# Third attention layer of a four-layer model: context projections ahead of the loop by way of DRAM, values one batch early, heads turned seven steps behind

## What is computed

```
ln_out = _ln(hidden_states, ln_w, ln_b)
q = _ln(_fp8_linear(ln_out, wq), qln_w, qln_b)      # 16 heads of 128
k = _ln(_fp8_linear(ln_out, wk), kln_w, kln_b)      # 8 heads of 128
v = _fp8_linear(ln_out, wv)                         # 8 heads
core = _gqa(q, k, v)                                # softmax(q k^T / sqrt(128)) v
qx = _ln(_fp8_linear(ln_out, wqx), qxln_w, qxln_b)
kvx = einsum('bsi,oi->bso', cond, w_kv_x)           # cond: the context, in f32
kx, vx = split(kvx, 2)                              # kx gets a layer norm per head
core_x = _gqa(qx, kx, vx)
y = fp8_linear(concat(core, core_x) * smoothing, wproj)
```

## Time and profile before

| | |
|---|---|
| median of the runs | 1834.83 us |
| the profiled execution, its own time | 1835.48 us |
| span, first to last instruction | 1833.7 us |
| PE busy | 1525.9 us (83%) |
| DVE busy | 1080.1 us (59%) |
| ACT busy | 804.5 us (44%) |
| POOL busy | 794.2 us (43%) |
| mean granted clock of TensorE | 0.871 |
| L2 attention, rounding stage | 864 to 899 us |
| L2 attention, main loop | 899 to 1307 us |

### The profile page before, as it was taken

One profiled execution on the slowest core, in us unless ns is written; L12 is line 12 of the kernel. 1 busy time (PEld: TensorE's weight loads), 2 busy tenths in 40 slices (PEclk: granted clock), 3 DMA queues, 4 the chain that ended last, 5 costly groups with the idle time before them and its releaser, 6 DMA issues. The chain is left out here.

```text
span 1833.7 us, 25059 instructions
## 1 busy us (share of the span) xinstructions
PE 1525.9 (83%) x8562; PEld 980.8 (53%) x8600; DVE 1080.1 (59%) x2317; ACT 804.5 (44%) x1879; POOL 794.2 (43%) x959
## 2 busy tenths in 40 slices
PE   7566659999797799997399999999799989836772
PEld 5222235656464365655167777777455555525661
DVE  7999961223674643355778888888722255462336
ACT  3989862110333211112488888888521112412221
POOL 3367641000200299791277777777210000027772
PEclk9655659999697999998699999999899988858796
DMA  2499871110504011320200000000111100156656
GB/s 78 89 177 182 172 162 33 36 42 18 184 2 167 27 48 65 115 66 25 68 2 1 1 1 1 1 1 1 44 30 43 35 25 1 46 195 233 231 171 238
DMA packets 174223, 140.12 MB, mean 76 GB/s; under 512 B 141793, under 2 KB 154721, under 8 KB 170386
## 3 DMA queue, kind: packets, MB, share of 16 engines
q1 hardware_dynamic: 165314, 114.89, 22.0%
q0 software_dynamic: 6416, 22.03, 3.6%
q10 hardware_dynamic: 2368, 1.61, 0.3%
HBM read 85.43 MB, written 19.50 MB: 57 GB/s over the span
## 5 line engine op out<-in xcount | busy, mean ns | idle before, releaser
L389 PE MATMUL l1e_gu<-x_normT,l1e_w 128*128 128x512 f32 x384 | 171.6, 602 | 0.0
L1859 POOL CAST l0m_pi<-l0m_pf 128x1024 bf16<-128x1024 int16 x128 | 133.2, 1040 | 87.0 <-ACT l0m_pf L1926 85.4
L1451 PE MATMUL l2x_pr<-l_w,l2x_xq 128*128 128x512 bf16 x538 | 133.6, 385 | 37.8 <-ACT credits L42 35.9
L1926 ACT ACTIVATE l0m_pf<-l0m_s,l0m_bias,l0x_sq 128x1024 int16<-128x1024 f32 x128 | 153.9, 1204 | 19.2 <-DVE l0m_bias L1957 12.6
L1953 DVE TENSOR_REDUCE l0m_mx<-l0m_s 128x1 f32<-128x1024 f32 x128 | 155.6, 1215 | 4.7 <-PE l0m_s L1868 4.4
L1868 PE MATMUL l0m_s<-l0x_kT,l0x_qT 64*128 64x512 bf16 x256 | 70.6, 575 | 64.7 <-ACT l0m_pf L1926 63.5
L389 PE MATMUL l0e_gu<-x_normT,l0e_w 128*128 128x512 f32 x272 | 121.3, 601 | 0.0
L1578 DVE BATCH_NORM_STATS2 l2x_bn<-l2x_raw 128x6 f32<-128x128 f32 x384 | 83.3, 279 | 64.3 <-ACT l2x_raw L1519 64.3
L389 PEld LDWEIGHTS l1e_gu<-x_normT,l1e_w 128*128 128x128 f32 x384 | 74.2, 194 | 84.2 <-issue 83.1
L389 PE MATMUL l2e_gu<-x_normT,l2e_w 128*128 128x512 f32 x256 | 114.3, 602 | 0.0
L441 ACT ACTIVATE l1e_sil<-l1e_gu 128x512 f32<-128x512 f32 x48 | 28.6, 596 | 178.6 <-PE l1e_gu L389 178.6
(11 more groups left out here) (505 smaller groups left out, 3608.1 us busy)
## 6 DMA issues: line engine op xcount, KB each, us to landing
l3m_w<-in_l_moe SPq DMA_DIRECT2D x16, 1280.0 KB, 6.9
l1e_w<-in_l_ffn SPq DMA_DIRECT2D x24, 384.0 KB, 3.1
l_rows<-zero_row SPq DMA_DIRECT2D x8, 1024.0 KB, 10.9
l_w<-l_rows SPq DMA_DIRECT2D x8, 1024.0 KB, 12.7
l0e_w<-in_l_ffn SPq DMA_DIRECT2D x17, 384.0 KB, 3.1
l2e_w<-in_l_ffn SPq DMA_DIRECT2D x16, 384.0 KB, 3.1
ctx_tok<-l_route SPq DMA_DIRECT2D x8, 512.0 KB
l2q_wps<-in_l_wp SPq DMA_DIRECT2D x16, 256.0 KB, 2.8
```

The costliest lines, as they stand in the source:

```text
L389: last = nc.tensor.matmul(gu[half][:, m, :], w[:, c % SW, (2 * k + m) * P:(2 * k + m + 1) * P], pg.xnT[:, k, cols(n)], start=(k == 0), sto ...
L1451: last = nc.tensor.matmul(flat(pr[t % 2][:]), src[:, k, tokens], pg.l2_w3[:, part, k, at:at + W], start=(k == 0 and part == 0), stop=(k == ...
L1859: nc.gpsimd.tensor_copy(pi[:, n % 8, :], pf[:, n % 4, :]).then_inc(s["rounded"], 1)
L1926: nc.scalar.activation(pf[:, n % 4, :], s_ps[n % 3][:], ACT.Exp, scale=sq[:, h, b:b + 1], bias=bias[:, n % 4:n % 4 + 1], accum_out=sm[:, b ...
```

## The change

- **Context projections move.** PE computes all 32 of them (8 batches, four parts of 512 columns: kx twice, vx twice) in the rounding stage, into eight PSUM banks. ACT copies each to one of four buffers `kv`, one behind each copy of output weights, and the last 18 after the rounds. POOL stores each to the DRAM tensor `l2_kv`.
- **SP loads them in the loop**, four loads of 256 KB per batch, into `kx` and `vx`, two batches deep, which lie where the weights `l2_wx` were.
- **Values one batch early.** Side 1 used steps 0 and 1 for kx and 6 and 7 for vx. Now its steps 0 and 1 project the v of the next batch, so steps 6 and 7 are without projection in every item but the first. The last item has none in steps 0 and 1 either. Statistics and normalization of kx read `kx` instead of `raw`.
- **Heads are turned at lag 7** instead of 6 on PE and ACT.

The diff, cut to its core:

```diff
+            @block.tensor
+            def _(pe):
+                for i in range(KV_STEPS):
+                    b, u = divmod(i, 4)
+                    if i >= 8:
+                        pe.wait_ge(kv_kept, i - 7)
+                    for k in range(KD):
+                        last = nc.tensor.matmul(kv_ps[i % 8][:], pg.ctxT[:, k, b * P:(b + 1) * P], pg.l2_wx[:, k, u * W:(u + 1) * W],
+                                                start=(k == 0), stop=(k == KD - 1))
+                    last.then_inc(kv_done, 1)
+
+            @block.gpsimd
+            def _(pool):
+                for i in range(KV_STEPS):
+                    pool.wait_ge(kv_kept, i + 1)
+                    pool.dma_start(pg.l2_kv[i], kv[:, i % 4]).then_inc(kv_stored[i % 4], 16)
+
+                def keep_kv(i):
+                    act.wait_ge(kv_done, i + 1)
+                    if i >= 4:
+                        act.wait_ge(kv_stored[i % 4], 16 * (i // 4))
+                    nc.scalar.activation(kv[:, i % 4], kv_ps[i % 8][:], ACT.Copy).then_inc(kv_kept, 1)
...
                             keep(q)
+                            keep_kv(q)
                 keep(14)
                 keep(15)
+                for i in range(14, KV_STEPS):
+                    keep_kv(i)
...
+            def source(it, t):
+
+                if t >= 6 or (it[1] == 1 and t < 2):
+                    return V_, it[0] + it[1], t % 2
+                return (QX if it[1] else K_ if t < 2 else Q_), it[0], None
+
+            def projects(it, t):
+                if it is None:
+                    return False
+                if t >= 6:
+                    return it == (0, 0)
+                return it != (B - 1, 1) or t >= 2
...
+            @block.sync
+            def _(sp):
+                for b in range(B):
+                    for i in range(4):
+                        sp.wait_ge(kv_stored[i], 16 * (b + 1))
+                    if b >= 2:
+                        sp.wait_ge(s["normed"], item((b - 2, 1)) * 6 + 2)
+                    for u in range(2):
+                        sp.dma_start(kx[:, b % 2, u], pg.l2_kv[4 * b + u].rearrange("p (j d) -> p j d", j=U)).then_inc(kx_in[b % 2], 16)
+                    if b >= 2:
+                        sp.wait_ge(s["valued"], item((b - 2, 1)) * 4 + 4)
+                    for u in range(2):
+                        sp.dma_start(vx[:, b % 2, u * W:(u + 1) * W], pg.l2_kv[4 * b + 2 + u]).then_inc(vx_in[b % 2], 16)
...
-                        if job := norm_due(t, 6, pi, ai):
+                        if job := norm_due(t, 7, pi, ai):
...
-                            dve.wait_ge(s["raw"], item(pi) * 8 + t + 3)
+                            if source(pi, t)[0] != V_:
+                                dve.wait_ge(s["raw"], projected(pi, t) + 3)
+                                rows = raw[:, t]
+                            else:
+                                dve.wait_ge(kx_in[pi[0] % 2], 16 * 2 * (pi[0] // 2 + 1))
+                                rows = kx[:, pi[0] % 2, t]
```

More of the change, by code:

```diff
@@ L1283, in attention_l2 @@
         wp_in = [pg.sem(f"l2q_wp_in{i}") for i in range(4)]
+        kv_done, kv_kept = pg.sem("l2q_kv_done"), pg.sem("l2q_kv_kept")
+        kv_stored = [pg.sem(f"l2q_kv_stored{i}") for i in range(4)]
+        KV_STEPS = 4 * B
         with ExitStack() as st:
@@ L1292, in attention_l2 @@
             wps = sb("wps", [P, 4, 2, D])
+            kv = sb("kv", [P, 4, W])
+            kv_ps = [st.enter_context(nc.psum_tensor(f"l2q_kv_ps{i}", [P, W], F32)) for i in range(8)]
             block = st.enter_context(nc.Block())
@@ L1441, in fn @@
                     for t in range(8):
[L1442 to L1457 removed]
+                        if projects(pi, t):
+                            pe.wait_ge(s["raw"], projected(pi, t) + 1)
+                            which, batch, part_v = source(pi, t)
+                            tokens = slice(batch * P, (batch + 1) * P)
+                            src = xq[:, which]
+                            at = 3072 + part_v * W if which == V_ else 4096 + (t - 2) * W if which == QX else t * W
+                            for k in range(KD):
+                                for part in range(3):
+                                    last = nc.tensor.matmul(flat(pr[t % 2][:]), src[:, k, tokens], pg.l2_w3[:, part, k, at:at + W],
+                                                            start=(k == 0 and part == 0), stop=(k == KD - 1 and part == 2))
                             last.then_inc(s["proj"], 1)
@@ L1512, in fn @@
                     for t in range(8):
[L1513 to L1519 removed]
+                        if projects(pi, t):
+                            act.wait_ge(s["proj"], projected(pi, t) + 1)
+                            which, batch, part_v = source(pi, t)
+                            dst = pg.xnT[:, batch % 2, part_v * W:(part_v + 1) * W] if which == V_ else flat(raw[:, t])
+                            nc.scalar.activation(dst, flat(pr[t % 2][:]), ACT.Copy, scale=scales[:, which:which + 1]).then_inc(s["raw"], 1)
                         if job := due(t, 3, ai, zi, wi):
```

51 lines of the change are left out of this document (21 added, 30 removed).

## The result

The changed kernel takes **1848.72 us** (median of 4 runs, 1846.66 to 1851.12), the kernel before 1835.04 beside it (4 runs, 1834.25 to 1835.59): a ratio of 1.0071, 95% interval 1.0058 to 1.0085. It is 13.7 us slower. 1821 was forecast, with 1805 to 1836 as the range.

What follows compares the result with a forecast made beforehand. PE was taken to bound the loop, every microsecond counting (24.35 us per item). +22.9 (rounding stage) - 2.8 - 5.7 - 23.9 - 4.3 (loop items) = -13.8 us, giving 1821 us, range 1805 to 1836.

Steps and rivals of the forecast that it cites:

- items 3 to 14: Steady main loop: 22.4 us per item instead of 24.39, together -23.9 us.
- PE's own work: Main loop: PE's work falls to 20.9 us per item, the lower bound of an item.
- The free steps: Steps 6 and 7, without projections: PE waits for ACT's copy of turned probabilities, 0.8 to 0.95 us beyond PE's work.
- DVE and POOL late for step 0: Steps 4 to 7 into step 0: late DVE statistics and POOL rstd delay the normalization of probabilities, 0.6 us per item.
- Meetings of DVE and POOL: Main loop: DVE and POOL block each other on the shared port more often, at most another 0.5 us per item.
- rival C: Loop steps 4 to 7: DVE and POOL become the bound; slower from 23.55 us per item, 1845 at 24.4; chance 0.13.
- The rounding stage: Ahead of the loop: 32 projections take 55.0 us of PE at full clock; stage 58.8 against 35.9 us, +22.9.
- D: Rounding stage: stores set the pace, ACT waiting for buffers and PE for banks; 10 us more, 1831; chance 0.12.
- E: Rounding stage: lower clock throughout, 110 us for the projections, +55 on the sum, 1876; chance 0.05.
- About 1 us at either end: Ends of the rounding stage: hand-over to the next block, about 1 us, beside the last copy and last store issue.
- Item 0 and items 1 and 2: Loop start: item 0 falls from 13.6 to 10.8 us (-2.8), items 1 and 2 from 43.15 to 37.5 (-5.7).
- Item 15: Last item: without projection in steps 0 and 1, 20.9 us instead of 25.2, -4.3; the end behind it stays.

Runs made afterwards that it cites:

- e11: Changed kernel with statistics of two of four heads (less DVE) and POOL's power made a product, together: 1829.32 us (one run), pair of items 43.96 us.
- e5: Changed kernel with less DVE work: statistics of two of four heads from the third item on; 1843.20 us (one run), pair of items 46.11 us.
- e6: Changed kernel with less POOL work: the power in the rstd sets becomes a product; 1834.74 us (one run), pair of items 45.13 us.
- e7: Changed kernel with less ACT work: four scaled copies of the output heads become one instruction; 1843.63 us (one run), pair of items 46.03 us.
- e8: Changed kernel with less PE work: one of four matmuls of each output part; 1851.67 us (one run), pairs of 46.87 to 48.38 us.
- e3: Changed kernel with the 32 stores issued from SP's queue instead of POOL's: 1843.70 us, ratio 1.0036 to the kernel before.
- e13: Kernel before with only the heads turned seven steps behind instead of six: 1834.97 us, ratio 0.9996 to the kernel before.
- e4: Changed kernel with only the 16 context value projections moved, keys projected in the loop: 1827.69 us, ratio 0.9956 to the kernel before.
- e9: Changed kernel with only the 16 context key projections moved, values projected in the loop: 1824.38 us, ratio 0.9933 to the kernel before.
- e1: Changed kernel with heads turned at lag 6 again instead of 7: 1849.61 us, ratio 1.0063 to the kernel before.

## Why the prediction was wrong

The step that failed is **items 3 to 14**, "22.4 per item", and in it the term for what comes late to step 0, "I put 0.6 on this". It measured 1.5 (1.16 for POOL, as foreseen, and 0.36 for ACT's copy of turned heads, not foreseen). The mechanism was right in the main and the term mis-sized: 0.9 of the 1.0 us per item that were missing. The item is half of the whole error: 12.3 of the 25 us between -13.8 and +11.4.

- *PE's own work*, 20.9 per item, held: e11, with DVE and POOL lightened, comes to 21.98 with one wait of 0.62 left, 0.8 in all; the remaining 21.2 is 0.3 above it.
- *The free steps*, "0.8 to 0.95 beyond PE's work": named rightly, the values' wait for ACT's copy is there in every item, 0.62 listed and about 0.8 in all. I took it from the end of the loop, where the listed wait is 0.69. One reading there was wrong: in the pair of steps that took 4.26 PE doesn't wait for probabilities but for ACT's copy of turned heads (below). Two similar sizes from two causes made it look like one.
- *DVE and POOL late for step 0*, "I put 0.6 on this": the place and the queue were right (POOL's normalization of probabilities, behind the third rstd set). The size was 0.97 listed, 1.16 in all, and 0.36 for the copy of turned heads beside it: 1.5. I showed no row for it and put a small number. The end of the loop before has rows of both waits, which I passed over; they show the places and not the size:

```profile
1281.57 0.63 PE L1471 MATMUL l2x_tr<-ident,l2x_raw 128*128 128x128 f32 x4 [0.52 <-ACT l2x_qT L1533]
1297.45 0.66 PE L1478 MATMUL l2x_pt<-ident,x_norm 128*128 128x128 f32 x4 [0.26 <-POOL x_norm L1434]
```

- *Meetings of DVE and POOL*, "at most another 0.5 per item": DVE's busy time over ten items of the steady loop is 207.0 us (1013.9 to 1248.4), before 204.4 (991.2 to 1234.7), so 0.3 per item.
- *The range of the sum*. The break-even that I worked out for rival C, 23.55 per item, was 1.15 above my value, a twentieth of an item; it got 0.13. What came is 23.44 without a bound engine. I had tied the slow outcome to "DVE and POOL become the bound"; it needs neither full (e5 to e8). That a chain over four engines is a little late at several links fits all but e8's side of it, and is argued, not shown.

*The rounding stage* (+22.9 forecast, +25.5): the 55.0 us of matmuls came out at 55.2 (866.93 to 922.1), at full clock, and neither ACT nor the stores held them; D and E fell, and a store took 2.3 us in the median (3.9 beside the rounding), issued in 0.54. The missing 2.6 us is the hand-over. "About 1 us at either end" assumed that a stage ends when its last DMA is issued; e3 shows that on POOL's queue it ended 3.3 us later.

*Item 0 and items 1 and 2* (-8.5 forecast, -4.0): PE's gap at the hand-over was 5.49 us, not 3, and the clock fell again (0.87 to 940), 1.8 us by e3; and items 1 and 2 pay the waits that the others pay, and once 1.73 for ACT's copy of turned heads (at 951.85).

*Item 15* (-4.3 forecast, +2.5): the sum left out what the lag costs at the end, 1.3 us (e13), and that an item with no projection in steps 0 and 1 is a row of waits, 1.48 and 0.97, behind which the clock fell to 0.50, twice.

*What wasn't asked.* The sum priced 32 projections as one thing at 1.72 us each, in the loop and in the stage. But the stage had 35.9 us free, room for 16 or so, and the 16 beyond cost 25.5 us, 1.6 each. In the loop the first 16 (the keys) bring 1.65 per pair, the next 0.15. The right question was what the seventeenth projection brings and costs; with it half of the change is a gain of 11.8 us, and the other half a loss of some 24. Numbers between 16 and 32 weren't run.

## What to carry to other kernels

When work moves from a full stage to an idle one, price the last unit that is moved, not the mean: it costs nothing while the idle time lasts and everything after, while its gain shrinks as soon as the full engine starts to wait. An engine that is 99% busy hides the waits for all the others; take its work away between two links of their chain and the waits show (0.88 gained for 3.44 taken, in e4), so take it from steps where no engine's answer is due (1.65 for the same 3.44, in e9). A run that lightens one engine at a time tells quickly whether that engine sets the pace; look also at which wait it shortened, since a queue's order can be what the saved work paid for (e7).

## What the runs showed of the hardware

- The clock can be lost inside a loop that keeps PE about 90% busy (43.9 of 48.1 us in e1, 41.9 of 46.9 in e8). It fell to 0.50 to 0.60 behind four of ten waits of 2.1 us (e1), behind three of nine pairs of waits of 0.84 and 0.97 (e8), and both times behind waits of 1.48 and 0.97 with 1.6 us between their ends (the end of the changed kernel). Each fall in e1 and e8 makes a pair 1.1 to 1.5 us longer. Waits of 0.2, 0.6 and 1.0 us in every item kept 1.00 (the changed kernel, 1013.9 to 1248.4). Taking work from PE saved nothing in the loop and brought three such falls, 4.3 us in all (e8).
- A block that issued DMAs from POOL's queue ended 3.3 us after its last issue (3.34 in the changed kernel); from SP's queue it didn't wait for them (0.75 us from the end of ACT's last copy to the next block's first instruction).
- Stores of 256 KB landed in 3.8 and 3.9 us on SP's and POOL's queue beside DVE's rounding and the loads of weights, and in 2.0 and 2.3 afterwards.
